# Motif terms of a Trainium2 kernel: neighbour planes replaced sixteen at a time by indirect gathers from DRAM, in place of a second buffer and moves within SBUF

## The chip, the cores and the metric

The kernel runs on one NeuronCore of one Trainium2 chip, as one program. The metric is the device time of one execution in microseconds (us). Data are float32 images of 2 x 128 x 128 x 96.

## What is computed

For each of the two images the reference adds a channel attention block to a group-normalised input, and then adds a "motif" block. Only the motif block bears on the change. It reads the image of shape 128 x 128 x 96 as 128 planes (feature channels) of 128 rows and 96 columns, in 16 groups of 8 planes:

```python
slices = [feature[:, :, ki:ki + Hm, kj:kj + Wm] for ki in range(K) for kj in range(K)]   # K = 3: nine shifts
patches = jnp.stack(slices, axis=2)
motif = patches.reshape(B, G, Cg * 9, L).reshape(B, G, 9, Cg, L)                         # G = 16, Cg = 8
gram = jnp.einsum('bgjcl,bgjdl->bgjcd', motif, motif)
...
nn_idx = jnp.argmin(d2, axis=-1)
u_max = jnp.max(nn_idx, axis=-1)
c_max = jnp.sum(nn_idx == u_max[..., None], axis=-1).astype(feature.dtype)
motif_nn = jnp.take_along_axis(motif, u_max[..., None, None], axis=3)
term = jnp.floor(motif * motif_nn * c_max[..., None, None] / Cg)
out_ser = motif * batch_mask + term
ser2 = out_ser.reshape(B, G, 9 * Cg, L).reshape(B, G, Cg, 9, Hm, Wm)
for k in range(K * K):
    ki, kj = (k // K, k % K)
    out = out.at[:, :, :, ki:ki + Hm, kj:kj + Wm].add(ser2[:, :, :, k])
```

The 72 patches of a group (9 shifts of 8 planes) are regrouped as nine blocks of eight. Each block picks one neighbour patch, which depends on the data. The last reshape counts the same 72 patches by plane and shift, so at output shift k, plane p takes the term of patch 9p + k, whose block is (9p + k) // 8 = p + (p + k) // 8. The block, and with it the neighbour plane, is the same for shift after shift, and changes once, at k = 8 - p.

## The kernel before, in words

For each of the two images (b = 0, 1) three stages follow one another: `attention`, `motif_grams` (the Gram matrices, the distances, and the choice of the neighbours) and `motif_terms` (the terms and their sum). A barrier stands between stages. The change lies in `motif_terms`.

**Layout.** Each of the 128 SBUF partitions holds one plane (partition 8g + p is plane p of group g). The planes lie in DRAM in `f_dram`. They are worked on in N = 8 slabs of R = 16 rows. Per slab there is `fc` (the plane's own rows, a plain load of 768 KB) and `near` (the neighbour plane's rows, 18 rows, gathered by an indirect DMA whose per-partition offset is in `index`). Both have four slots, by slab modulo 4.

**Steps.** `steps` takes slabs in pairs: for a pair (2m, 2m + 1) it runs shift 0 of both slabs, then shift 1 of both, up to shift 8. These are 72 steps an image, numbered n. Step n and step n - 2 are the same slab at neighbouring shifts. Each step takes:

- VectorE, `product` (L1510): `prod` = shifted `fc` times `near`; and two steps later `overshoot` (L1611): `over` = (scale times `prod`) < `rnd`. The order on VectorE is product n, overshoot n - 2, product n + 1, and so on (`LAG` = 2).
- ScalarE, two activations (L1637, L1642) that round the scaled product to `rnd`.
- TensorE, 8 fp32 matmuls with the identity (L1663) and 4 bf16 matmuls with minus the identity (L1667), which sum `rnd` and `over` in PSUM.
- After shift 8 ScalarE copies the slab's sum out (`finish`, L1629), and GpSimd adds it to the output in DRAM with an accumulating DMA (`add_out`, L1563), at shift 2 of the next pair but for the last pair.

**The neighbour planes.** At shift `sh` the 16 partitions 8 - sh + 8g need another neighbour plane than before. The kernel gathers both: `near` with the first pick, and a second full buffer `near2` with the second pick. Before each step of shift 1 to 8 SyncE waits for the product of step n - 2 (`product_made`), then issues a DMA within SBUF from `near2` to `near` for those 16 partitions (L1541, 108 KB). `product_inputs` makes product n wait for it on `moved`. The gathers (`gather`, L1555) of slab i + 2 are issued by GpSimd after the products of slab i at shifts 1 and 3 (the two halves of `near`) and 5 and 7 (the two halves of `near2`). SyncE's queue also holds the `fc` loads (L1528) of slab i + 2, at shift 5. The first two slabs' `near` and `near2` are gathered whole as the stage begins.

All of SyncE's DMAs go out in the order of its program, and so do GpSimd's: each waits behind what stands ahead of it in its engine's list. `on_pool` is False for every step, so that GpSimd only issues DMAs here (and two small memsets).

Of the kernel before, what the change touches and what calls it, by code (L numbers as in the profile page):

```python
# [1013 lines left out]
def motif_grams(nc, b, k, img, x_after, f_dram, x1_rows, x1_out, att_sems, sems):  # L1014
# [15 lines left out]
    with ExitStack() as ctx:  # L1030
# [23 lines left out]
        sel = sb("sel", [MG, 6, KK], F32)  # L1054
        block_picks = sb("block_picks", [MG, 3, KK], F32)
        both = sb("both", [P, 2, 3, KK], F32)
# [390 lines left out]
def motif_terms(nc, b, k, x, f_dram, out, gram_sems):  # L1447
# [10 lines left out]
    with ExitStack() as ctx:  # L1458
        sb = lambda n, s, d: ctx.enter_context(nc.sbuf_tensor(f"{n}{b}", s, d))
        sem = lambda n: ctx.enter_context(nc.semaphore(f"{n}{b}"))  # L1460
        near = sb("near", [P, SLOTS, NR * C], F32)
        near2 = sb("near2", [P, SLOTS, NR * C], F32)
        fc = sb("fc", [P, SLOTS, R * C], F32)
# [6 lines left out]
        scale = sb("scale", [P, KK], F32)  # L1470
        index = sb("index", [P, 2, 2, N], I32)
        acc = [ctx.enter_context(nc.psum_tensor(f"acc{s}_{b}", [P, R // BR, 512], F32)) for s in range(2)]
        (own, scaled, indexed, edged, prod_v, prod_p, rm_done, rnd_done, over_done, acc_done, out_ready) = (
            sem(n) for n in ("t_dve", "scaled", "indexed", "edged", "prod_v", "prod_p", "rm_done",
                             "rnd_done", "over_done", "acc_done", "out_ready"))
        stored, near_in, near2_in, fc_in = ([sem(f"{n}{j}_") for j in range(SLOTS)]
                                            for n in ("stored", "near_in", "near2_in", "fc_in"))
        moved = [sem(f"moved{s}_") for s in range(2)]
# [9 lines left out]
        def product_made(eng, n):  # L1488

            eng.wait_ge(prod_p if on_pool[n] else prod_v, sum(p == on_pool[n] for p in on_pool[:n + 1]))  # L1490
# [34 lines left out]
        @block.sync  # L1525
        def _(sp):
            def load_rows(dst, src, i, sem_):
                sp.dma_start(dst[:, i % SLOTS, :], src[:, R * i * C:(R * i + R) * C]).then_inc(sem_[i % SLOTS], 16)  # L1528

            if b + 1 < B:  # L1530
                for s_ in gram_sems.values():
                    sp.sem_clear(s_)
            for i in range(2):
                load_rows(fc, f_dram, i, fc_in)
            for n, (i, sh) in enumerate(steps):
                if sh >= 1:

                    if sh == 1:
                        sp.wait_ge(near2_in[i % SLOTS], landings(i))
                    product_made(sp, n - 2)  # L1540
                    sp.dma_start(near[MC - sh:P:MC, i % SLOTS, run(i)], near2[MC - sh:P:MC, i % SLOTS, run(i)]  # L1541
                                 ).then_inc(moved[i % 2], 16)
                if sh == 5 and i + 2 < N:
                    if i >= 2:
                        product_made(sp, number[(i - 2, KK - 1)])
                        product_made(sp, number[(i - 2, KK - 2)])
                    load_rows(fc, f_dram, i + 2, fc_in)
            for j in range(SLOTS):
                sp.wait_ge(stored[j], 16 * (N // SLOTS))

        @block.gpsimd
        def _(pool):
            def gather(i, second, cells, h=0):
                s = i % SLOTS
                pool.indirect_dma_start(  # L1555
                    (near2 if second else near)[:, s, cells], None, f_dram.rearrange("y (e o) -> (y e) o", o=1),
                    bass.IndirectOffsetOnAxis(ap=index[:, second, h, i:i + 1], axis=0)
                ).then_inc((near2_in if second else near_in)[s], 16)

# [7 lines left out]
            pool.wait_ge(indexed, 1)  # L1567
            for second in range(2):
                gather(0, second, run(0))
                gather(1, second, run(1))  # L1570
            pool.wait_ge(indexed, 2)
            for n, (i, sh) in enumerate(steps):
                if sh in (1, 3, 5, 7) and i + 2 < N:
                    product_made(pool, n)
                    if sh == 1 and i + 2 == N - 1:
                        nc.gpsimd.memset(near[:, (i + 2) % SLOTS, R * C:NR * C], 0.0).then_inc(edged, 1)
                    h = sh // 2 % 2
                    gather(i + 2, sh // 4, part_run(i + 2, h), h)
                if i >= 2 and sh == 2:
                    add_out(i - 2)  # L1580
                if on_pool[n]:
                    product_inputs(pool, n)
                    product(nc.gpsimd, n).then_inc(prod_p, 1)
# [4 lines left out]
        def _(dve):  # L1588
# [4 lines left out]
            for h in range(2):  # L1593
                nc.vector.scalar_tensor_tensor(index[:, :, h, :], offset[:, :].unsqueeze(2).to_broadcast([P, 2, N]),  # L1594
                                               float(HALF * C * h),
                                               k["row_base"][:, :].unsqueeze(1).to_broadcast([P, 2, N]), ALU.add,
                                               ALU.add).then_inc(indexed, 1)

# [73 lines left out]
def build(nc, x, w_qkv, b_qkv, w_dw, b_dw, temperature, w_out, b_out, out):  # L1672
# [5 lines left out]
    with ExitStack() as ctx:  # L1678
# [5 lines left out]
            minus_round=sb("minus_round", [P, 1], F32), group_planes=sb("group_planes", [MG, P], F32),  # L1684
            own_block=sb("own_block", [P, 2, KK], F32), pick=sb("pick", [P, 2, 3], F32),
            same_head=sb("same_head", [C, C], F32), same_block=sb("same_block", [MR, MR], F32),
# [45 lines left out]
```

## Time and profile before

| | us |
|---|---|
| median of 3 runs (lowest to highest) | 1575.14 (1575.06 to 1578.28) |
| the profiled execution, its own time | 1579.09 |
| span of its profile | 1577.1 |
| `motif_terms` of image 0 in it | about 513 to 788 |
| `motif_terms` of image 1 in it | about 1304 to 1577 |

The profile is that of one execution. Its time and its span differ by 2.0 us, which lie around the span. Engines are named PE (TensorE matmul), PEld (its weight load), DVE (VectorE), ACT (ScalarE), POOL (GpSimd) and SP (SyncE); a q behind a name is the engine's sequencer. An L with a number is a line of the kernel. "near<-near" is the move from `near2` to `near`, as the trace leaves numbers off the names of buffers. In a list of instructions, the part in brackets is the time that the engine was idle before it, and what ended the idle time.

### The profile page before, as it was taken

How to read it: one execution, taken by the hardware profiler on the slowest of the kernel's cores; microseconds unless marked ns; L12 is line 12 of the kernel's file. 1: busy time of each engine (PE TensorE's matmuls, PEld its weight loads, DVE VectorE, ACT ScalarE, POOL GpSimd, SP SyncE). 2: the span in 40 equal slices, each digit the busy share in tenths (PEclk: the TensorE clock that was granted, in tenths of full speed). 3: DMA queues.
4: the chain of work that ended last, by engine and by line, in shares of the span. 5: the costliest groups of instructions: out<-in, count | busy, mean ns of one | idle time of the engine just before them, and what ended most of it. 6: DMA issues, size and time to landing. Idle time of an engine off the chain costs nothing. (4 is left out here: it accounts for less than half of the span.)

```text
span 1577.1 us, 33962 instructions
## 1 busy us (share of the span) xinstructions
PE 1338.1 (85%) x13569; PEld 1079.0 (68%) x13569; DVE 1144.1 (73%) x1903; ACT 879.2 (56%) x950; POOL 680.3 (43%) x680
## 2 busy tenths in 40 slices
PE   0799999996988699999767887889978986999996
PEld 0699887985987355555356777888968983555553
DVE  8577675468864699999645565663786856999995
ACT  1455563212541699999634444542215526999995
POOL 3698892452220335440057566752533303354400
PEclk9999999898999799999969898997989997999998
DMA  6366631792141546453236655423901415464432
GB/s 224 88 209 203 195 90 32 212 273 93 42 168 75 180 123 178 100 142 72 52 101 182 182 155 169 126 62 101 273 5 70 193 62 172 131 178 100 142 72 51
DMA packets 78850, 208.12 MB, mean 132 GB/s; under 512 B 15633, under 2 KB 19827, under 8 KB 76035
## 3 DMA queue, kind: packets, MB, share of 16 engines
q1 hardware_dynamic: 64228, 153.09, 31.5%
q0 software_dynamic: 7296, 40.08, 9.9%
q10 hardware_dynamic: 7168, 12.78, 3.0%
q8 instruction: 107, 1.75, 0.5%
q14 instruction: 51, 0.42, 0.1%
HBM read 89.39 MB, written 67.04 MB: 99 GB/s over the span
## 5 line engine op out<-in xcount | busy, mean ns | idle before, releaser
L1663 PE MATMUL acc<-rnd,ident 128*128 128x376 f32 x1152 | 391.6, 483 | 24.7 <-ACT rnd L1642 24.7
L886 PE MATMUL ps_a<-wa,xa 128*128 128x192 f16 x1536 | 305.3, 251 | 12.7 <-DVE y_s L615 12.5
L1663 PEld LDWEIGHTS acc<-rnd,ident 128*128 128x128 f32 x1152 | 216.5, 192 | 145.3 <-ACT rnd L1642 26.0
L886 PE MATMUL ps_a<-wb,xb 128*128 128x192 f16 x1536 | 303.7, 250 | 0.0
L1510 DVE TENSOR_TENSOR prod<-fc,near 128x1504 f32<-128x1504 f32 x144 | 247.3, 1717 | 33.1 <-DMA near<-f_planes,index 17.4
L1637 ACT ACTIVATE rnd_m<-prod,plus_round,scale 128x1504 f32<-128x1504 f32 x144 | 235.8, 1637 | 61.6 <-DVE prod L1510 51.0
L549 POOL TENSOR_TENSOR vt<-z 96x256 f32<-96x256 f32 x248 | 256.6, 1055 | 18.7 <-ACT z L790 18.6
L1611 DVE SCALAR_TENSOR_TENSOR over<-prod,scale,rnd 128x1504 bf16<-128x1504 f32 x144 | 255.5, 1777 | 0.0
L1555 POOL DMA_INDIRECT near<-f_planes,index x56 | 159.0, 2840 | 209.8 <-DVE prod L1510 201.8
L1642 ACT ACTIVATE rnd<-rnd_m,minus_round 128x1504 f32<-128x1504 f32 x144 | 223.2, 1550 | 4.8
L886 PEld LDWEIGHTS ps_a<-wa,xa 128*128 128x128 f16 x1536 | 154.1, 100 | 19.7 <-issue 18.2
L886 PE MATMUL ps_a<-wfb,xb 128*128 128x96 f16 x1536 | 159.4, 207 | 1.7 <-issue 1.7
L886 PE MATMUL ps_a<-wfa,xa 128*128 128x96 f16 x1536 | 159.4, 208 | 1.2 <-issue 1.2
L886 PEld LDWEIGHTS ps_a<-wb,xb 128*128 128x128 f16 x1536 | 154.0, 100 | 0.9 <-issue 0.2
L557 POOL TENSOR_TENSOR td<-side 128x192 f32<-128x192 f32 x128 | 99.0, 774 | 120.5 <-ACT side L808 120.5
L886 PEld LDWEIGHTS ps_a<-wfa,xa 128*128 128x128 f16 x1536 | 141.8, 99 | 0.6 <-issue 0.6
L886 PEld LDWEIGHTS ps_a<-wfb,xb 128*128 128x128 f16 x1536 | 139.7, 99 | 2.3 <-issue 2.2
L1149 ACT ACTIVATE turned_hi<-ps_m 126x768 f16<-126x768 f16 x102 | 79.9, 810 | 90.9 <-PE ps_m L1200 90.9
L886 PE MATMUL ps_a<-wc,xc 102*128 102x192 f16 x512 | 128.8, 251 | 0.0
L1667 PE MATMUL acc<-over,minus_ident 128*128 128x376 bf16 x576 | 117.0, 326 | 8.8 <-DVE over L1611 8.6
L609 DVE TENSOR_TENSOR td<-side 128x192 f32<-128x192 f32 x128 | 73.9, 577 | 66.7 <-ACT side L808 63.6
L815 ACT ACTIVATE qk<-y_s 128x384 f16<-128x384 f32 x128 | 66.9, 523 | 92.0 <-DVE y_s L615 92.0
(304 smaller groups left out, 2390.3 us busy)
## 6 DMA issues: line engine op xcount, KB each, us to landing
xb<-xa ACTq DMA_DIRECT2D x64, 195.0 KB, 2.7
f_planes<-img SPq DMA_DIRECT2D x8, 1536.0 KB, 14.0
fc<-f_planes SPq DMA_DIRECT2D x16, 768.0 KB, 5.5
out<-done_rows POOLq DMA_DIRECT2D x16, 768.0 KB, 8.2
v_a<-xa SPq DMA_DIRECT2D x40, 260.0 KB, 2.7
v_b<-xb SPq DMA_DIRECT2D x40, 260.0 KB, 3.2
xa<-v_a SPq DMA_DIRECT2D x40, 260.0 KB, 4.9
xb<-v_b SPq DMA_DIRECT2D x40, 260.0 KB, 5.5
```

The costliest lines, as they stand in the source:

```text
L549: last = nc.gpsimd.tensor_tensor(out[:, i], row(p_), row(q_), op)
L557: nc.gpsimd.tensor_tensor(td[:, n % 2, 0], side[:, n % 2, 0], side[:, n % 2, 1], ALU.add).then_inc(t_made, 1)
L609: nc.vector.tensor_tensor(td[:, s, 1], side[:, s, 0], side[:, s, 1], ALU.subtract).then_inc(d_made, 1)
L886: mm = lambda a, w, first, end: nc.tensor.matmul(out(i), a, w, start=first, stop=end)
L1149: last = nc.scalar.activation(columns(turned_hi[q % 2], col), six(ps_hi[u % 2]), ACT.Copy)
L1510: return vec.tensor_tensor(prod[:, n % PRODS], fv, nv, ALU.mult)
L1555: pool.indirect_dma_start((near2 if second else near)[:, s, cells], None, f_dram.rearrange("y (e o) -> (y e) o", o=1), bass.IndirectOffset ...
L1611: nc.vector.scalar_tensor_tensor(over[:, n % 2], prod[:, n % PRODS], scale[:, sh:sh + 1], rnd[:, n % RNDS], ALU.mult, ALU.is_lt).then_inc( ...
L1637: nc.scalar.activation(rnd_m[:, n % 2], prod[:, n % PRODS], ACT.Identity, bias=k["plus_round"][:, 0:1], scale=scale[:, sh:sh + 1]).then_in ...
L1642: nc.scalar.activation(rnd[:, n % RNDS], rnd_m[:, n % 2], ACT.Identity, bias=k["minus_round"][:, 0:1]).then_inc(rnd_done, 1)
L1663: nc.tensor.matmul(o(m), k["ident"][:, :], rnd[:, n % RNDS, BR * m:BR * m + BR, :], start=False, stop=False, skip_group_check=True)
L1667: last = nc.tensor.matmul(o(m), k["minus_ident"][:, :], over[:, n % 2, BR * m:BR * m + BR, :], start=False, stop=(sh == KK - 1), skip_grou ...
```

## The change

`near2` and the moves go. The planes that change at a shift are gathered from DRAM by GpSimd, 16 at a time, straight into their rows of `near`. The offsets of these gathers are in a new table `index2` with 16 partitions (one per group), 8 columns by shift and one value for each slab, which VectorE computes at the start of the stage from `block_picks`; that tensor becomes a global one. The gathers of slab i + 2 are now two (at shifts 2 and 5), each placed behind the replacement of the same step, and no longer wait for product n. SyncE keeps only the `fc` loads.

```diff
-        block_picks = sb("block_picks", [MG, 3, KK], F32)
+        block_picks = k["block_picks"]
...
-        near2 = sb("near2", [P, SLOTS, NR * C], F32)
...
-        index = sb("index", [P, 2, 2, N], I32)
+        index = sb("index", [P, 2, N], I32)
+        index2 = sb("index2", [MG, MC, N], I32)
+        base2 = sb("base2", [MG, 2], F32)
+        offset2 = sb("offset2", [MG, MC], F32)
...
@@ @block.sync
             for n, (i, sh) in enumerate(steps):
-                if sh >= 1:
-
-                    if sh == 1:
-                        sp.wait_ge(near2_in[i % SLOTS], landings(i))
-                    product_made(sp, n - 2)
-                    sp.dma_start(near[MC - sh:P:MC, i % SLOTS, run(i)], near2[MC - sh:P:MC, i % SLOTS, run(i)]
-                                 ).then_inc(moved[i % 2], 16)
                 if sh == 5 and i + 2 < N:
...
@@ @block.gpsimd
+            planes = f_dram.rearrange("y (e o) -> (y e) o", o=1)
+
+            def gather(i, cells, h=0):
+                pool.indirect_dma_start(near[:, i % SLOTS, cells], None, planes,
+                                        bass.IndirectOffsetOnAxis(ap=index[:, h, i:i + 1], axis=0)
+                                        ).then_inc(near_in[i % SLOTS], 16)
+
+            def replace(i, sh):
+
+                lines = slice(MC - sh, P, MC)
+                pool.indirect_dma_start(near[lines, i % SLOTS, run(i)], None, planes,
+                                        bass.IndirectOffsetOnAxis(ap=index2[:, MC - sh, i:i + 1], axis=0)
+                                        ).then_inc(moved[i % 2], 16)
...
             pool.wait_ge(indexed, 1)
-            for second in range(2):
-                gather(0, second, run(0))
-                gather(1, second, run(1))
-            pool.wait_ge(indexed, 2)
+            gather(0, run(0))
+            gather(1, run(1))
+            pool.wait_ge(indexed, 3)
             for n, (i, sh) in enumerate(steps):
-                if sh in (1, 3, 5, 7) and i + 2 < N:
-                    product_made(pool, n)
-                    if sh == 1 and i + 2 == N - 1:
+                if sh >= 1:
+                    product_made(pool, n - 2)
+                    replace(i, sh)
+                if sh in (2, 5) and i + 2 < N:
+                    if sh == 2 and i + 2 == N - 1:
                         nc.gpsimd.memset(near[:, (i + 2) % SLOTS, R * C:NR * C], 0.0).then_inc(edged, 1)
-                    h = sh // 2 % 2
-                    gather(i + 2, sh // 4, part_run(i + 2, h), h)
+                    gather(i + 2, part_run(i + 2, sh // 5), sh // 5)
                 if i >= 2 and sh == 2:
                     add_out(i - 2)
...
@@ @block.vector
             for h in range(2):
-                nc.vector.scalar_tensor_tensor(index[:, :, h, :], offset[:, :].unsqueeze(2).to_broadcast([P, 2, N]),
-                                               float(HALF * C * h),
-                                               k["row_base"][:, :].unsqueeze(1).to_broadcast([P, 2, N]), ALU.add,
-                                               ALU.add).then_inc(indexed, 1)
+                nc.vector.tensor_scalar(index[:, h, :], k["row_base"][:, :], offset[:, 0:1], float(HALF * C * h),
+                                        ALU.add, ALU.add).then_inc(indexed, 1)
+            c.then_wait(nc.vector.tensor_scalar(base2[:, 0:1], k["plane_f"][0:MG, :], float(MC * PLANE), None, ALU.mult))
+            nc.vector.scalar_tensor_tensor(base2[:, 1:2], k["group_base"][0:MG, :], float(MC), base2[:, 0:1], ALU.mult,
+                                           ALU.add)
+            c.then_wait(nc.vector.scalar_tensor_tensor(offset2[:, :], k["block_picks"][:, 0, 1:KK], float(PLANE),
+                                                       k["block_picks"][:, 1, 1:KK], ALU.mult, ALU.add))
+            for i in range(N):
+                last = nc.vector.tensor_scalar(index2[:, :, i], offset2[:, :], base2[:, 1:2], float(first_row(i) * C),
+                                               ALU.add, ALU.add)
+            last.then_inc(indexed, 1)
```

## Rows read from the trace of the kernel before

**Rows 1.** The page: span, and the engines in 40 equal slices.
```profile
span 1577.1 us, 33962 instructions
...
PE   0799999996988699999767887889978986999996
...
DVE  8577675468864699999645565663786856999995
```
**Rows 2.** Busy time by stretch, in the steady part of each `motif_terms`.
```profile
core 0: us, PE busy (x) PEld busy (x) DVE busy (x) ACT busy (x) POOL busy (x), PEclk, DMA share, GB/s
...
1322.00:1564.00 242.00, 238.37 (x883) 132.24 (x883) 234.81 (x141) 230.32 (x147) 82.21 (x32) 1.00 0.42 110
532.00:775.00 243.00, 237.87 (x879) 131.68 (x878) 235.25 (x141) 230.93 (x147) 81.56 (x31) 1.00 0.42 110
```
**Rows 3.** What DVE waited for, 510 to 788, then 1304 to 1577 us.
```profile
DVE prod L1510 <- DMA near<-f_planes,index: 9.6, 2, 8.2
DVE prod L1510 <- DMA near<-near: 8.6, 5, 2.9
...
DVE prod L1510 <- DMA near<-f_planes,index: 7.8, 2, 7.4
DVE prod L1510 <- DMA near<-near: 7.0, 5, 3.1
```
**Rows 4.** Line L1541, the moves: issue to landing, whole span.
```profile
L1541 SPq DMA_DIRECT2D near<-near x128: 486/487/531, 527.5 to 1549.1; - x128
...
DMA to landing us min/median/max: 2.0/2.2/7.3
```
**Rows 5.** Instructions in order of time, DVE and POOL, 1333 to 1342 us.
```profile
1334.67 1.77 DVE L1611 SCALAR_TENSOR_TENSOR over<-prod,scale,rnd 128x1504 bf16<-128x1504 f32 x1
1335.02 3.88 POOL L1555 DMA_INDIRECT near<-f_planes,index  x1 [7.75 <-DVE prod L1510]
1336.36 1.71 DVE L1510 TENSOR_TENSOR prod<-fc,near 128x1504 f32<-128x1504 f32 x1
...
1338.00 1.77 DVE L1611 SCALAR_TENSOR_TENSOR over<-prod,scale,rnd 128x1504 bf16<-128x1504 f32 x1
1339.20 3.02 POOL L1555 DMA_INDIRECT near<-f_planes,index  x1 [0.30 <-issue]
1339.69 1.71 DVE L1510 TENSOR_TENSOR prod<-fc,near 128x1504 f32<-128x1504 f32 x1
```
**Rows 6.** The same view, POOL alone: DVE idle, then image 0's second gather after step 2.
```profile
1309.09 0.94 POOL L1555 DMA_INDIRECT near<-f_planes,index  x1 [0.30 <-issue]
...
535.53 2.26 POOL L1555 DMA_INDIRECT near<-f_planes,index  x1 [1.07 <-DVE prod L1510]
```
**Rows 7.** The same view, 1388 to 1402 us: a gather beside a DVE gap.
```profile
1388.88 1.95 POOL L1563 DMA_DIRECT2D out<-done_rows  x2
...
1394.63 1.78 DVE L1611 SCALAR_TENSOR_TENSOR over<-prod,scale,rnd 128x1504 bf16<-128x1504 f32 x1
...
1394.99 2.39 POOL L1555 DMA_INDIRECT near<-f_planes,index  x1 [4.17 <-DVE prod L1510]
...
1397.64 1.73 DVE L1510 TENSOR_TENSOR prod<-fc,near 128x1504 f32<-128x1504 f32 x1 [1.23 <-DMA near<-near]
```
**Rows 8.** Line L1555 in 535 to 536 us: one half gather, its landing from issue.
```profile
L1555 POOL DMA_INDIRECT near<-f_planes,index x1: 2259/2259/2259, 535.5 to 535.5; - x1
...
DMA to landing us min/median/max: 5.4/5.4/5.4
```
**Rows 9.** Busy time by stretch around two adds and the third and fourth gathers, image 0.
```profile
598.00:602.00 4.00, 4.00 (x18) 2.48 (x17) 4.00 (x4) 3.97 (x3) 3.31 (x3) 1.00 0.77 194
602.00:606.00 4.00, 4.00 (x16) 2.38 (x15) 4.00 (x3) 3.93 (x4) 0.51 (x1) 1.00 0.93 187
606.00:608.00 2.00, 2.00 (x10) 1.09 (x9) 0.91 (x1) 2.00 (x2) 1.88 (x1) 1.00 1.07 242
608.00:610.00 2.00, 2.00 (x9) 1.25 (x8) 0.81 (x1) 1.81 (x2) 0.00 (x0) 1.00 1.05 230
610.00:612.00 2.00, 0.79 (x3) 0.19 (x1) 2.00 (x2) 1.05 (x1) 0.81 (x1) 1.00 0.79 245
```
**Rows 10.** The tile `index`: the DVE operations that write it.
```profile
L1594 DVE SCALAR_TENSOR_TENSOR index<-offset,row_base x4: 166/172/176, 513.6 to 1304.8; 128x16 int32<-128x16 f32 x4
```

More of the change, by code:

```diff
@@ L1475, in motif_terms @@
                              "rnd_done", "over_done", "acc_done", "out_ready"))
-        stored, near_in, near2_in, fc_in = ([sem(f"{n}{j}_") for j in range(SLOTS)]
-                                            for n in ("stored", "near_in", "near2_in", "fc_in"))
+        stored, near_in, fc_in = ([sem(f"{n}{j}_") for j in range(SLOTS)] for n in ("stored", "near_in", "fc_in"))
         moved = [sem(f"moved{s}_") for s in range(2)]
@@ L1552, in _ @@
         def _(pool):
[L1553 to L1558, printed above, removed]
+            planes = f_dram.rearrange("y (e o) -> (y e) o", o=1)
[8 more added lines that the diff above has]
+                                        ).then_inc(moved[i % 2], 16)
             def add_out(i):
@@ L1684, in build @@
             minus_round=sb("minus_round", [P, 1], F32), group_planes=sb("group_planes", [MG, P], F32),
-            own_block=sb("own_block", [P, 2, KK], F32), pick=sb("pick", [P, 2, 3], F32),
+            own_block=sb("own_block", [P, 2, KK], F32), block_picks=sb("block_picks", [MG, 3, KK], F32), pick=sb("pick", [P, 2, 3], F32),
             same_head=sb("same_head", [C, C], F32), same_block=sb("same_block", [MR, MR], F32),
```

## The prediction

> **What bounds the kernel now.** I read the page first, for the two stretches where DVE and PE are both near 9 tenths [rows 1]: these are the two `motif_terms` stages. Busy time by stretch then shows that in 242 us PE is busy for 238.4, DVE for 234.8 and ACT for 230.3, at full granted clock, while POOL is busy for 82 [rows 2]. Three engines run in step, and none has room to catch up: what DVE loses, PE loses too, and the end moves by as much. The list of instructions gives the cadence: product to product 3.33 us (1336.36 to 1339.69), and from a product's end (1338.07) to the next product's start 1.62 us, in which one `over` runs [rows 5]. The waits say what DVE lacks beside that: 9.6 and 7.8 us for the first gathers of a stage, and 8.6 and 7.0 us for the moves [rows 3]. The moves are nearly always hidden: they land 2.2 us after their issue [rows 4], and product n starts 1.62 + 3.33 = 4.95 us after the end of product n - 2, which releases its move. **So 4.95 us is the whole room** from product n - 2 to the landing of what product n needs. The question is what a gather on POOL takes of it.
>
> **What is removed.** 64 moves an image, with the waits for them: 8.6 us in image 0 and 7.0 in image 1, 15.6 in all. 28 gather issues an image become 14, which were off the path (POOL idle for most of the stage). Half of the gathered bytes come back as the 64 replacements of 108 KB, so DRAM traffic is unchanged; with a DMA share of 0.42 [rows 2] I give the freed SBUF traffic nothing.
>
> **What is added, off the path.** DVE gets 11 more small operations at the stage's start; the one that writes `index` takes 0.17 us [rows 10], so some 2 us with their waits. They stand behind the operation that releases the first gather, in the 7.4 to 8.2 us that DVE waits for it [rows 3]: nothing. Without that cover they would cost these 2 us an image.
>
> **What is added, on the path: the replacement's issue.** With DVE idle an indirect issue takes 0.94 us. With DVE busy it takes 3.88 us from 1335.02 to 1338.90, and the next 3.02 us, from 1339.20 to 1342.22. Both end 0.82 us after the end of a product (1338.07, 1341.40) [rows 5, 6]. Where DVE pauses, one takes 2.39 us and ends at 1397.38, 0.97 us after the `over` that ended at 1396.41 [rows 7]. The two direct DMAs of the adds take 0.98 us each beside a busy DVE [rows 7]. I read this as follows: the issue must read its list of offsets, gets no turn while DVE runs one instruction on the heels of the last, gets one at a product's end or in a pause, and then needs 0.8 us. How much of that goes with the number of partitions no row shows; bounds are 0 and 0.97, and I take 0.8, since all issues seen, of whole and half gathers, need about that.
>
> **From the issue's end to the landing.** A half gather (442 KB) lands 5.4 us from its start, 5.4 - 2.26 = 3.1 after the issue's end [rows 8]. A move (the same 16 partitions and bytes, but on SP and from SBUF) lands 2.2 - 0.49 = 1.7 after [rows 4]. These are the bounds; I take 2.0, nearer to the move, which has the same size. By the Trainium skill, page "DMA: Bandwidth & Descriptors", section "Anatomy of one DMA — SWDGE (gpsimd) path", a DMA from GpSimd costs 2.0 us plus its bytes at 436 GB/s; an estimate from it is 2.25 us here, and each wait below would be 0.25 us longer. No run here shows it.
>
> **The steady wait.** Replacement n is issued after product n - 2, so POOL starts under `over`, misses the boundary behind it, and gets its turn at the end E of product n - 1. It lands at E + 0.8 + 2.0 = E + 2.8, where product n could have started at E + 1.62: DVE waits 1.2 us. This wait is a pause. Replacement n + 1, already queued, gets its turn in it, behind the `over`: it is done at about E + 1.7 + 0.8 and lands at E + 4.5, before product n + 1 is due at E + 2.8 + 3.33. So every second step waits: 32 of an image's 64, and 32 x 1.2 = 38.4 us. By the bounds (0 + 1.7 and 0.97 + 3.1, less 1.62) a wait is 0.1 to 2.4 us.
>
> **The queue at shift 2.** POOL's list is now replacement, gather, add for the even slab, and then the same for the odd one. The odd slab's replacement stands behind 442 KB and an add, and shares their queue. How long: around the adds the DMA engines are full from 600 to 611 us [rows 9], some 11 us for two adds, a gather and the last part of another (1.5 us each), so some 4 us an add. In image 0 a move on its own queue waited up to 7.3 us there [rows 4]. POOL finishes the first add's issue at about E + 3.6; gather and add occupy the queue to about E + 8.0; the replacement behind lands at E + 10.0 (2.0 later), where its product was due at E + 2.8 + 3.33 = E + 6.1: 3.9 us. The next one, behind the second gather and add, costs 2.6. Less the 1.2 counted already, that is 5.3 for two pairs of slabs, and 1.5 for the last, which has no gathers: 12 us an image. Bounds: 0, if the queue doesn't hold the replacement back, and 20.
>
> **The start.** SP, rid of its waits, issues `fc` loads 2 and 3 at once, beside the second gather; against that `near2` no longer stands before the first replacement. I take 1 us lost, between a gain of 2 and a loss of 3.
>
> **Sum.** Image 0: 38.4 + 12 + 1 - 8.6 = +42.8. Image 1: 38.4 + 12 + 1 - 7.0 = +44.4. Together +87 on a span of 1577.1 and an own time of 1579.1. On the median, 1575.1, that gives **1662 us**. A measurement of this kernel can tell about 0.2% (3 us) from no change. With the waits at 0.3 us and the queue's cost halved it is 1575 + 2 x (10 + 6 + 1) - 16 = 1593; with 2.0 us and 16 us, 1575 + 2 x (64 + 16 + 1) - 16 = 1721.
>
> **Rival 1: the turn comes at the end of whatever DVE runs.** Then an issue starting 0.28 us after a product's end is through behind the `over`, in 2.26 us as at 535.53 [rows 6], and lands at 0.28 + 2.26 + 2.0 = 4.5 us, inside 4.95. No steady wait; the queue at shift 2 and the start stay: 2 x 13 - 15.6 = +10, 1586 us. For it: that one row. Against it: 3.88 us in the steady rows [rows 5], where the issue went past the end of an `over` at 1336.44. This is also what the Trainium skill says on the page "SBUF — State Buffer", section "Who interferes with whom": a VectorE instruction with two SBUF inputs contends with a GpSimd one that reads SBUF, and the second blocks until the first finishes. By that rule the trace agrees that DVE's instructions hold the issue up, and disagrees on where it ends. Chance 0.17.
>
> **Rival 2, the other side: faster.** The issue for 16 partitions is cheap. It decides at 4.95 - 0.28 - 2.0 = 2.67 us of issue: below that nothing waits in the steady part; and if a queued replacement also passes beside the adds, all waits for moves are gone and nothing replaces them: 1575.1 - 15.6 = 1559.5 us. For it: the 0.94 us with DVE idle, and the few rows at 2.3 [rows 6, 7]. Against: the steady rows, and that it must hold in both places. Chance 0.11.
>
> **Rival 3: every step waits.** If the pause gives POOL no turn, or a landing takes 3 us and more, both slabs' replacements are late: 2 x (64 x 1.2 + 13) - 15.6 = +164, 1739 us. Against it: the pause at 1396.41 did give a turn [rows 7]. Chance 0.07. My forecast has 0.65.
>
> **Range and chances.** 1580 to 1710 leaves out rival 2, rival 3 and the edge of rival 1, some 2 in 10. Faster comes from rival 2, 0.11; within 0.2%, 0.03, from the bounds of rival 1; slower 0.86.
>
> **What would show it.** Right: DVE waits for `near` from an indirect DMA some 30 times an image, 1.2 us each, mostly ahead of even slabs' products; indirect issues of two kinds, near 3.8 and near 2 us; POOL busy for over half of the stage; two waits of 2 to 4 us at shift 2 of pairs 2 to 4. Wrong: issues of 16 partitions well under 2 us beside a busy DVE (rival 2), all near 2.3 us (rival 1), waits at odd slabs as well (rival 3), or a granted clock below full in the steady part, which I have priced at nothing because a PE pause of over a microsecond left it at 1.00 [rows 9].

## The result and the profile after

The changed kernel takes 1610.69 us (median of 4 runs, 1609.07 to 1613.03) against 1575.1 us (4 runs of the kernel before on the same chip): a ratio of 1.0235, 95% interval 1.0194 to 1.0277. It is slower by some 36 us, where 87 were forecast. The profiled execution took 1609.07 us, with a span of 1607.3.

The page of the changed kernel, its span and two engines in 40 slices (compare [rows 1]):

```profile
span 1607.3 us, 33940 instructions
...
PE   0799999996985989899568877989959958988996
...
DVE  8577774588843989899544554763786839988985
```

Busy time by stretch, changed kernel, in 243 and 250 us of the two stages (compare [rows 2]):

```profile
532.00:775.00 243.00, 229.85 (x829) 125.79 (x828) 224.27 (x135) 220.21 (x140) 143.98 (x78) 0.98 0.31 80
1340.00:1590.00 250.00, 234.59 (x851) 130.38 (x849) 229.74 (x138) 224.41 (x143) 144.48 (x78) 0.98 0.31 78
```

PE, DVE and ACT each lose 8 to 11 us of the 243; POOL rises from 82 to 144. The DMA share falls from 0.42 to 0.31, as the moves are gone. DVE's waits, 510 to 790, then 1303 to 1607 us (compare [rows 3]):

```profile
DVE prod L1511 <- DMA near<-f_planes,index: 29.1, 14, 6.5
...
DVE prod L1511 <- DMA near<-f_planes,index: 30.7, 13, 7.9
```

Before, they were 18.2 and 14.8 in all. A `motif_terms` stage, counted from DVE's first operation in it (`offset`) to the end of its barrier, took 275.1 and 272.6 us before (547.7 together) and takes 291.4 and 291.8 (583.2); "stages" below gives this sum. **So the stages lose 35.5 us**: 26.8 in DVE's waits, 4.0 at the barriers (below), 4.7 elsewhere. Of these 4.7 us, 3.3 are the changed kernel's additional small operations of DVE at the start, 1.6 us in image 0 and 1.7 in image 1 (from `offset` to the last `scale` 0.9 us before, 2.5 here): they stand where DVE had waited for the first gather, whose wait is counted shorter by them. The untouched stages vary between single executions (1029.4 before, 1024.1 here, 1012 to 1030 over all the profiles), so single executions are compared by this stage sum.

Where the 29.1 us of image 0 stand: 10.5 at the start (6.50, 2.24, 1.42, 0.36), 15.6 at shifts 2 and 3 of pairs 2 to 4 (3.80 + 2.69, 4.53 + 2.24, 1.36 + 1.00), 2.6 at shift 1 of the same pairs (0.84, 0.93, 0.85), and 0.3 more. The steady part, for which 38.4 us were forecast, has nothing. Instructions in order of time there, changed kernel, DVE and POOL:

```profile
558.93 1.77 DVE L1619 SCALAR_TENSOR_TENSOR over<-prod,scale,rnd 128x1504 bf16<-128x1504 f32 x1
559.28 2.13 POOL L1557 DMA_INDIRECT near<-f_planes,index  x1 [1.19 <-DVE prod L1511]
560.62 1.72 DVE L1511 TENSOR_TENSOR prod<-fc,near 128x1504 f32<-128x1504 f32 x1
```

The replacement's issue begins 0.35 us into an `over`, as the gather at 1335.02 in [rows 5] did, but is through at 561.41, 0.71 us after the end of that `over` (560.70), where the gather went on to 0.82 us after the next product. The line's summary, whole span:

```profile
L1557 POOL DMA_INDIRECT near<-f_planes,index x128: 847/2134/3770, 518.9 to 1578.8; - x128
...
DMA to landing us min/median/max: 2.6/4.0/8.2
```

With 0.28 + 4.0 = 4.3 us the median landing is inside the room of 4.95.

### The profile page after: what moved, and what is told of

It reads as the page before. It is cut to its first block and busy times, and to the rows that moved or that the text cites. A ratio compares the mean times of both kernels' runs of the same rounds, so it can differ in the third digit from the quotient of the medians.

```text
span 1607.3 us, 33940 instructions
## 1 busy us (share of the span) xinstructions
PE 1342.4 (84%) x13569; PEld 1077.6 (67%) x13569; DVE 1148.5 (71%) x1925; ACT 880.3 (55%) x950; POOL 816.4 (51%) x780
## 5 line engine op out<-in xcount | busy, mean ns | idle before, releaser
L1671 PE MATMUL acc<-rnd,ident 128*128 128x376 f32 x1152 | 398.6, 490 | 26.8 <-ACT rnd L1650 26.8
L1557 POOL DMA_INDIRECT near<-f_planes,index x128 | 254.5, 1988 | 212.0 <-DVE prod L1511 201.3
L1671 PEld LDWEIGHTS acc<-rnd,ident 128*128 128x128 f32 x1152 | 220.7, 195 | 151.0 <-ACT rnd L1650 28.1
L886 PE MATMUL ps_a<-wa,xa 128*128 128x192 f16 x1536 | 307.8, 253 | 12.7 <-DVE y_s L615 12.2
L1675 PEld LDWEIGHTS acc<-over,minus_ident 128*128 128x128 bf16 x576 | 48.1, 99 | 124.7 <-DVE over L1619 95.4
```

The lines of the kernel that those rows point to most:

```text
L886: mm = lambda a, w, first, end: nc.tensor.matmul(out(i), a, w, start=first, stop=end)
L1557: pool.indirect_dma_start(near[lines, i % SLOTS, run(i)], None, planes, bass.IndirectOffsetOnAxis(ap=index2[:, MC - sh, i:i + 1], axis=0)) ...
L1671: nc.tensor.matmul(o(m), k["ident"][:, :], rnd[:, n % RNDS, BR * m:BR * m + BR, :], start=False, stop=False, skip_group_check=True)
L1675: last = nc.tensor.matmul(o(m), k["minus_ident"][:, :], over[:, n % 2, BR * m:BR * m + BR, :], start=False, stop=(sh == KK - 1), skip_grou ...
```

## The experiments

**Is it the order in which products are released?** In the changed kernel a replacement lands, and so releases its product, only while the `over` ahead of that product runs; in the kernel before the move lands earlier. First, the kernel before with its moves released later:

```diff
                     product_made(sp, n - 2)
+                    if n >= 4:
+                        sp.wait_ge(over_done, n - 3)
                     sp.dma_start(near[MC - sh:P:MC, i % SLOTS, run(i)], near2[...]
```

> The kernel before, in which SyncE issues the move for step n only once overshoot n - 4 is done as well, 1.7 us later than now; the move then lands some 4.1 us after the end of product n - 2, still ahead of the 4.95 us at which product n is due. Theory A (order of release: GpSimd gets its turn at the first end of a VectorE instruction at which VectorE's next one had not yet been released when GpSimd asked): the next product is now released only after GpSimd asked, so the half gathers' issues fall from 3.0 and 3.9 us to about 2.3 and 1.5 us. Theory B (issues over 16 partitions are quicker than issues over 128): nothing changes, 3.0 and 3.9 us. Time by either within 10 us of the kernel before.

1591.16 us, stages 568.0: DVE waited 17.0 us for moves in each image, so the time isn't within 10 us of before, as both theories had it (22 more). The gathers were mixed. POOL's list, this kernel:

```profile
543.13 3.89 POOL L1557 DMA_INDIRECT near<-f_planes,index  x1 [8.42 <-DVE prod L1510]
547.33 3.03 POOL L1557 DMA_INDIRECT near<-f_planes,index  x1 [0.30 <-issue]
556.46 2.26 POOL L1557 DMA_INDIRECT near<-f_planes,index  x1 [6.10 <-DVE prod L1510]
```

So 128 partitions can be quick too, and neither theory predicts the mixture. What the three rows leave out: behind the third one's `over` DVE paused (its next product, at 558.86, waited 0.97 us for a move), behind the first two it didn't. Second, the changed kernel with its replacements sent to a spare tile that nothing waits for:

```diff
-            else:
-                eng.wait_ge(moved[i % 2], 16 * (8 * (i // 2) + sh))
...
-                pool.indirect_dma_start(near[lines, i % SLOTS, run(i)], None, planes,
+                if 8 * (i // 2) + sh > 1:
+                    pool.wait_ge(moved[i % 2], 16 * (8 * (i // 2) + sh - 1))
+                pool.indirect_dma_start(spare[lines, i % 2, run(i)], None, planes,
```

> The changed kernel, but the 16 planes are gathered into a spare buffer that nothing reads, and the products do not wait for them (the planes that change at a shift are thus left out of the result). Same issues, same partitions, same bytes. Theory A: products are released early, GpSimd loses its turn at the end of the overshoot, and the issues over 16 partitions take about 3.8 and 3.0 us in place of 2.1. Theory B: they stay at 2.1 us. VectorE's waits fall to those for the first two gathers, some 9 us an image; time about 1610 - 2 x 20 = 1570 us.

1570.49 us, stages 543.4, so the issues and their traffic cost next to nothing by themselves: the loss is in who waits. (The waits are 12.2 us below those of the kernel before and the barriers 4.0 above, which with the 3.3 us of small operations makes 542.8.) In image 0 the issues that began 0.35 us into an `over` took 2.13 us through pair 0, and from 585.80 on most took 3.02 to 3.77, with the same 16 partitions and with products released equally early in both. Release order and the number of partitions therefore can't be what makes the difference.

```profile
552.49 2.14 POOL L1558 DMA_INDIRECT spare<-f_planes,index  x1 [1.19 <-DVE prod L1510]
...
585.80 3.77 POOL L1558 DMA_INDIRECT spare<-f_planes,index  x1 [7.86 <-DVE prod L1510]
589.88 3.03 POOL L1558 DMA_INDIRECT spare<-f_planes,index  x1 [0.30 <-issue]
```

**The queue at shift 2.** No adds for slabs 0 to 5, nor the waits for them:

```diff
-                if i >= 2 and sh == 2:
-                    add_out(i - 2)
```

> The changed kernel without the accumulating DMAs of slabs 0 to 5 of each image (those slabs lack the motif sum in the output); the last two adds stay. Theory (queue at shift 2: the replacement stands behind gather and add on GpSimd's queue): VectorE's waits at shifts 2 and 3 of pairs 2 to 4 (15.6 and 16.9 us) go, as a half gather alone costs 0 to 0.4 us; time about 1610 - 32 = 1578 us. Rival (the gathers, or the issue times on GpSimd, make these waits): at least a third of them, 10 us over both images, stays, 1588 us or more.

1575.79 us, stages 550.5: 32.7 us less, and the waits at shifts 2 and 3 of pairs 2 to 4 are gone but for 0.3 us. In the changed kernel this is the stretch. POOL and DVE in order of time:

```profile
590.97 1.02 POOL L1564 DMA_DIRECT2D out<-done_rows  x1
592.29 1.94 POOL L1557 DMA_INDIRECT near<-f_planes,index  x1 [0.30 <-issue]
594.53 1.48 POOL L1550 DMA_INDIRECT near<-f_planes,index  x1 [0.30 <-issue]
596.00 1.01 POOL L1564 DMA_DIRECT2D out<-done_rows  x1
597.32 0.92 POOL L1557 DMA_INDIRECT near<-f_planes,index  x1 [0.30 <-issue]
598.94 1.73 DVE L1511 TENSOR_TENSOR prod<-fc,near 128x1504 f32<-128x1504 f32 x1 [3.80 <-DMA near<-f_planes,index]
...
605.05 1.73 DVE L1511 TENSOR_TENSOR prod<-fc,near 128x1504 f32<-128x1504 f32 x1 [2.69 <-DMA near<-f_planes,index]
```

The replacement issued at 597.32 took only 0.92 us of POOL, in DVE's pause, but its line's summary gives its landing at 7.7 us: 6.8 after the issue's end, where 1.7 to 1.9 is usual. It stands behind 768 KB of add. Cutting each add in four keeps the work and spreads it:

```diff
-                if i >= 2 and sh == 2:
-                    add_out(i - 2)
+                if i >= 2 and sh in (3, 4, 6, 7):
+                    add_out(i - 2, 4 * (3, 4, 6, 7).index(sh), 4)
```

> The changed kernel with each add of slabs 0 to 5 cut in four (4 rows, 192 KB each), issued at shifts 3, 4, 6 and 7, behind that step's replacement, not beside the half gathers of shifts 2 and 5. Theory (queue): a quarter of an add holds its queue for about 1 us, against the 0.7 us that a replacement has to spare, so most of the 32.5 us of waits at shifts 2 and 3 goes; 0 to 0.5 us is left for each quarter. Time about 1611 - 28 = 1583 us, still slower than the kernel before by 0.2 to 1%. Rival (the number of bytes in the queue matters, not where they stand): the waits spread out and stay, 1600 us or more. The barrier at a stage's end lags the last landing by 1.5 us with 36 DMAs of GpSimd in a stage and 3.5 with 86; if it goes by their number, it is about 4.2 us here with 104.

1578.83 us, ratio to before 1.0033 (1.0006 to 1.0059), stages 553.3: the waits at shifts 2 and 3 are gone here too, and the change is then worth nothing, or slightly less. The same cut in the kernel before (at shifts 2, 4, 6, 8, behind product n):

> The kernel before with each add of slabs 0 to 5 cut in four, issued at shifts 2, 4, 6 and 8 after the product of the step (its half gathers stand at 1, 3, 5 and 7). If the adds' load on the DMA engines is what makes the moves at shifts 2 to 4 late (5.7 and 4.0 us of waits), most of these waits go: 7 to 9 us faster than the kernel before, ratio 0.994 to 0.996, 1566 us beside a median of 1575. If the moves are late for another cause: no change. The barrier's lag by the number of GpSimd DMAs (54): 2.2 us, against 1.5.

1568.06 us, ratio 0.996 (0.993 to 0.999), stages 541.9: **faster than both kernels**, than the one before by 0.4%. The waits for moves behind the start fall from 5.7 to 1.8 us in image 0 and from 4.0 to 1.9 in image 1. DVE's waits in this kernel, 510 to 800:

```profile
DVE prod L1510 <- DMA near<-near: 4.7, 3, 2.8
DVE prod L1510 <- DMA near<-f_planes,index: 9.7, 2, 8.2
```

**The start.** `fc` loads 2 and 3 held back until product (i, 4):

> The changed kernel, but SyncE issues the fc loads of slabs 2 and 3 only after the products of slabs 0 and 1 at shift 4, as late as in the kernel before. If the early loads slow the second gather, VectorE's wait before its second product (2.2 and 2.1 us) falls to the 1.4 and 0.4 us of the kernel before, and the waits of the next two products shrink too: 2 to 4 us less over both images, about 1607 us. If not, the same as the changed kernel, 1610 us, with the same waits.

1599.98 us, but stages 583.1, the same as 583.2, so the rest of the difference in time is in the untouched stages (1015.0 against 1024.1). The early loads did slow the first gathers: held back, the second product's wait fell from 2.24 to 1.13 us and from 2.05 to 0.31, and in image 1 the first gather landed 8.4 us after `offset` instead of 10.4, and the first product came at 8.47 instead of 10.45. All waits of the start together fell from 10.5 to 8.0 and from 10.9 to 8.7 us. But new waits at shift 5 (1.1 and 1.6 us) and growth in others took as much. Not a lever.

**How near the edge is it?** A memset on POOL ahead of each replacement, 1000 and then 2000 elements a partition (0.93 and 1.8 us):

```diff
                     product_made(pool, n - 2)
...
+                    nc.gpsimd.memset(pad[:, :], 0.0).then_inc(padded, 1)
...
                     replace(i, sh)
```

> The changed kernel with a GpSimd memset of 128 x 1000 fp32 (about 0.9 us) between the wait for product n - 2 and the replacement of step n, so that GpSimd asks for its turn 0.9 us later, after the previous replacement has landed and the next product has been released, but still before the end of the overshoot. Theory A: it loses the turn at the end of the overshoot; the issue ends after the next product, 1.7 us later, and VectorE waits 1 us or more at every second step: some 30 us or more an image, 1670 us. Rival (the turn always comes at the end of the overshoot): the memset is covered by the overshoot, and the time stays within 10 us of 1610.

1616.19 us, stages 596.2. The issue begins 1.2 us into an `over` and is still through behind it, although its product had been released before it asked: by release order it should have lost this turn, and the time been near 1670. The 13 us more are further waits of DVE, 0.8 to 0.9 us each, most of them at steps where a gather also stands in POOL's list. DVE and POOL in order of time:

```profile
539.84 1.78 DVE L1626 SCALAR_TENSOR_TENSOR over<-prod,scale,rnd 128x1504 bf16<-128x1504 f32 x1
541.06 1.27 POOL L1560 DMA_INDIRECT near<-f_planes,index  x1 [0.15 <-POOL pad L1580]
543.31 0.93 POOL L1580 MEMSET pad<- 128x1000 f32 x1 [0.98 <-DVE prod L1514]
```

> As the kernel with the memset ahead of each replacement, but 128 x 2000 (1.8 us), so that GpSimd asks only about 0.5 us after the overshoot's end, while the next product runs. Then the forecast's regime must come about whatever decides a turn within the overshoot: the issue ends 0.7 us after the end of product n - 1, lands at E + 0.7 + 1.8 = E + 2.5 where product n was due at E + 1.6, and VectorE waits 0.9 us at every second step or more often: 25 to 60 us an image above the changed kernel's waits, 1660 to 1730 us. If the time stays within 10 us of the changed kernel, the room of 4.95 us is not what bounds a replacement.

1722.4 us, stages 698.2: now the request falls just behind the `over`, the turn comes at the product's end, and 58 of an image's 72 products wait, most of them 0.7 to 1.0 us. That is near the forecast's 1.2 for an issue that gets its turn there (with 0.71 and 1.9 us for its 0.8 and 2.0 it is 0.71 + 1.9 - 1.62 = 1.0). Instructions in order of time, POOL and DVE; the issue ends at 658.84, 0.72 us behind the product's end (658.12):

```profile
653.75 1.78 DVE L1626 SCALAR_TENSOR_TENSOR over<-prod,scale,rnd 128x1504 bf16<-128x1504 f32 x1
656.39 1.73 DVE L1514 TENSOR_TENSOR prod<-fc,near 128x1504 f32<-128x1504 f32 x1 [0.86 <-DMA near<-f_planes,index]
656.51 2.33 POOL L1560 DMA_INDIRECT near<-f_planes,index  x1 [0.16 <-POOL pad L1580]
658.03 1.78 DVE L1626 SCALAR_TENSOR_TENSOR over<-prod,scale,rnd 128x1504 bf16<-128x1504 f32 x1
660.69 1.73 DVE L1514 TENSOR_TENSOR prod<-fc,near 128x1504 f32<-128x1504 f32 x1 [0.88 <-DMA near<-f_planes,index]
```

A missed turn is therefore as dear as forecast. What was wrong is that it is missed.

**Why 3.88 us before and 2.13 after?** I sorted the indirect issues of the profiles by how long ago the last one had ended. Of those that begin 0.35 us into an `over` that a product follows without a pause, the kernel before has 18 that come 6.1 to 12.8 us after it: all 18 go past the end of the `over`. It has 6 that come up to 3.3 us after it: all 6 are through behind it. The changed kernel has 6 with 7.85 us, all long, and 75 with up to 4.2 us, all short. The 7.85 us are the two steps of shift 0, without a replacement; the issue behind them is the one at shift 1 that costs 0.8 to 0.9. Changed kernel, POOL and DVE in order of time:

```profile
579.46 3.77 POOL L1557 DMA_INDIRECT near<-f_planes,index  x1 [7.85 <-DVE prod L1511]
585.05 1.72 DVE L1511 TENSOR_TENSOR prod<-fc,near 128x1504 f32<-128x1504 f32 x1 [0.84 <-DMA near<-f_planes,index]
```

Four runs set out to test this (theory C in the expectations).

```diff
+            def touch():
...
+                if touches[0] > 0:
+                    pool.wait_ge(touched, 16 * touches[0])
+                pool.indirect_dma_start(spare[0:MG, ...], None, planes, ...).then_inc(touched, 16)
...
+                if sh == 0 and n >= 2:
+                    product_made(pool, n - 2)
+                    touch()
```

> The changed kernel, with one tiny indirect DMA (16 x 96 elements into a spare tile) added at each step of shift 0, behind product n - 2, where POOL otherwise issues nothing for 7.85 us. Theory C (recency): an indirect issue that starts under an over gets its turn at that over's end if POOL's last indirect issue ended within about 4.2 us, and only at the next product's end if it ended 6 us ago or more; in the kernel before 6 of 6 and 18 of 18 issues go by this, in the changed one 75 of 75 and 6 of 6. Then the six issues of 3.77 us become 2.13, their waits of 0.8 to 0.9 us go (5.2 us in all), and the two stages take 583 - 5 + 0.5 (the barrier's 6 more DMAs) = 579 us. Rival (it is the shift 1, or its place in the code, that makes the issue long): 3.77 us and the waits stay, 583 us and more.

> The kernel before, with the same tiny indirect DMA behind the product of every step at which GpSimd issues no gather, so that POOL has a turn every 3.3 us. Theory C: all gathers of 128 partitions issue in about 2.25 us, none in 3.88; the time stays within 10 us of the kernel before, as these issues are off the path. Rival (gathers of 128 partitions into near and near2 miss the over's end for another reason): 3.88 us as before, 18 times.

> The changed kernel with the adds in four parts at shifts 3, 4, 6 and 7 and the tiny indirect DMAs at shift 0. Theory C: the waits of 13.5 and 14.5 us of the version with split adds lose 2.6 each; against that some 0.3 us a stage for the barrier's additional DMAs: stages 553.3 - 4.6 = 549 us, the same as the kernel before (547.7 and 0.2% either way). Rival: 553 to 554.

1611.92 us (ratio 1.0282, 1.0227 to 1.0337), 1586.65 and 1574.92 (ratio 1.004, 1.0016 to 1.0063); stages 584.3, 565.1 and 548.5. The first two missed: waits at shift 1 stayed in part (0.91, none and 0.23 us in image 0), and gathers of the second took 3.15 and 3.02 us. My tiny issues waited for the landing of the one before and so started late, with the gathers queued behind them, some 1.1 us into an `over`. These two don't decide. The third met its number, but with two of image 0's three waits at shift 1 still there (0.87 us each), so that is partly luck. The fourth thins the turns out:

```diff
                     product_made(pool, n - 2)
-                    replace(i, sh)
+                    if sh % 2 == 0 and i % 2 == 0:
+                        replace(i, sh)
```

> The changed kernel that keeps only the replacements of even slabs at shifts 2, 4, 6 and 8, so that 13.3 us lie between them (or 6.66 from a gather at shift 5); the other 48 of an image's 64 are left out, and the terms that need them are not the reference's. Theory C: those at shifts 2, 4 and 8 take 3.77 us (those behind a gather less than 4.2 us ago 2.13), land late, and DVE waits 0.8 to 0.9 us for each such one: some 3 a pair, 12 an image, so about 10 us an image for 16 replacements, though POOL does a quarter of the work. Rival (fewer issues can only be quicker): all 2.13 us, no wait but those at shifts 2 and 3 behind the adds.

1585.08 us, stages 561.3. Image 0 has 12 long issues and 12 waits behind its start, 0.74 to 1.02 us each and 10.6 in all: as theory C had it in number and sum, and in place too but for one: none at shift 2 of the first pair, which is in the stage's start, and one at shift 6 of the last, which has no gather at shift 5. (They begin 0.5 us later in the `over`, so "long" is 3.28.) Three of the four short ones follow a gather by 1.1 us, the other is in the stage's start. POOL in order of time, this kernel (the first row is a gather):

```profile
547.35 2.25 POOL L1550 DMA_INDIRECT near<-f_planes,index  x1 [1.07 <-DVE prod L1511]
550.68 2.15 POOL L1557 DMA_INDIRECT near<-f_planes,index  x1 [1.08 <-DVE prod L1511]
564.51 3.28 POOL L1557 DMA_INDIRECT near<-f_planes,index  x1 [11.68 <-DVE prod L1511]
585.35 3.26 POOL L1557 DMA_INDIRECT near<-f_planes,index  x1 [17.56 <-DVE prod L1511]
```

Then the tiny issues again, each into a slot of its own, without waits:

> As the version with tiny indirect DMAs at the steps of shift 0, but each goes into a slot of its own, so that it doesn't wait for the landing of the one before (that wait had put its start off by 1.5 us and queued the next replacement behind it). Theory C: an issue that starts under an over gets its turn at the over's end if the turn before was also at an over's end and less than 4.4 us ago (698 of 698 issues so far). Then the six issues of 3.77 us become 2.13, the waits of 0.8 to 0.9 us at shift 1 go (5.2 us in all), and the stages take 583 - 5 + 0.5 = 579 us. Rival (the place in the code or the shift): 3.77 us and the waits stay.

> The kernel before with tiny indirect DMAs behind the product of every step without a gather, each into a slot of its own and without waits. Theory C: after the start of the stage the issues of gathers, 3.88 us long 18 times before, take 2.25 us. Rival (gathers of 128 partitions miss the over's end for another reason): 3.88 us, 18 times.

> The changed kernel with the adds in four parts and the tiny unwaited indirect DMAs at shift 0. Theory C: the waits of 13.5 and 14.5 us of the version with split adds become 11 to 12, against 0.3 us a stage for the barrier: stages 549 us, the time 4 us below that version's 1578.8, still not below the kernel before. Rival: stages 553.

In the first (1604.76 us, stages 582.3) no issue takes over 2.5 us any more and the waits at shift 1 are gone; DVE's waits fall by 2.6 us in all, not 5.2, as other waits grew, and the stages by 0.9, not 4. So the length of the issues came out as theory C had it, the time did not. POOL at the place of the 3.77:

```profile
578.20 2.15 POOL L1572 DMA_INDIRECT spare<-f_planes,index  x1 [1.19 <-DVE prod L1514]
581.53 2.14 POOL L1560 DMA_INDIRECT near<-f_planes,index  x1 [1.18 <-DVE prod L1514]
```

In the second, the kernel before, all 56 gathers are short; first its own list, then its line's summary:

```profile
537.95 2.27 POOL L1558 DMA_INDIRECT near<-f_planes,index  x1 [1.17 <-DVE prod L1513]
541.28 2.27 POOL L1558 DMA_INDIRECT near<-f_planes,index  x1 [1.06 <-DVE prod L1513]
```

```profile
L1558 POOL DMA_INDIRECT near<-f_planes,index x56: 938/2265/2296, 506.8 to 1472.6; - x56
```

The same gathers to the same tiles take 2.27 us if a turn precedes them, and 3.9 if none does. One run gave 1565.28 us, stages 551.0: nothing gained in them, as these issues were off the path, and 3.3 us lost, as much as the barrier takes for 47 more DMAs a stage (below). The third took 1580.0 us (ratio 1.0005, 0.9967 to 1.0043), stages 549.1 as expected; the 4 us in time are within its spread. The best form of the change is level with the kernel before and behind it with split adds (541.9).

**The barrier.** Line L1458, the end of the stage, changed kernel:

```profile
L1458 POOLq DRAIN  x2: 11053/11856/12658, 786.0 to 1596.0; - x2
L1458 SPq COMPARE_BRANCH  x2: 33/33/33, 795.2 to 1603.6; - x2
L1458 SPq DRAIN  x2: 7/7/7, 795.4 to 1603.8; - x2
L1458 SPq EVENT_SEMAPHORE  x2: 17/17/17, 798.8 to 1607.3; - x2
```

SP is past its last wait for a store at 795.2, and the barrier opens 3.6 us later, behind POOL's drain. Before, it opened 1.6 us after:

```profile
L1458 SPq COMPARE_BRANCH  x2: 33/33/33, 786.9 to 1575.4; - x2
L1458 SPq EVENT_SEMAPHORE  x2: 17/17/17, 788.5 to 1577.0; - x2
```

Over the kernels this lag goes with the DMAs that GpSimd issued in the stage: 1.6 us at 36, 2.3 at 54 (split adds before), 3.4 at 80, 3.6 at 86, 4.4 at 104, so about 0.04 us each. The version with sparse replacements, which is the changed kernel with 38, has 1.7.

## Why the prediction was right and wrong

**The bound** was right: with three engines in step, what DVE waited was lost (26.8 of the stages' 35.5 us), and the room of 4.95 us decided. The version with the longer memset lost some 0.9 us at most steps as soon as it was exceeded.

**"The steady wait" is the step that failed.** It said that POOL "misses the boundary behind it, and gets its turn at the end E of product n - 1". In the changed kernel the turn comes at the end of the `over`, and the landing inside the room; 38.4 us an image became 2.6, at shift 1 of three pairs. The step took 3.88 us [rows 5] as what an issue beside a busy DVE costs, and the row at 535.53 with 2.26 [rows 6] as the exception. The bracket of each row had the difference: 7.75 us idle ahead of the one, 1.07 ahead of the other. The forecast's own pattern, an issue every 3.3 us, is that of the second row.

**The issue's fixed part and the landing** were near: 0.71 us behind the boundary for 16 partitions (0.8 forecast), 1.7 to 1.9 us from issue end to landing where nothing stood ahead of it (2.0 forecast), 2.0 to 2.5 behind a half gather. The Trainium skill, page "DMA: Bandwidth & Descriptors", section "Anatomy of one DMA — SWDGE (gpsimd) path", gave an estimate of 2.25; the runs lie below it if counted, as there, from the issue's end; from the start of an issue with DVE idle, at 522.35, the landing came after 2.7.

**The queue at shift 2** was right in mechanism and size: 3.9 and 2.6 us forecast twice, 3.80 + 2.69 and 4.53 + 2.24 measured. Only the subtraction of "the 1.2 counted already" went with the failed step: 15.6 and 16.9 us instead of 12.

**The start** was forecast at about 2 us gained in waits (the 2.9 and 3.1 us of the moves there go, 1 is lost). Image 0 gained 2.0; image 1 gained nothing, and its first product came 10.45 us after `offset` where it had come after 8.25 (9.00 against 9.10 in image 0). The version with late `fc` loads shows why: without `fc` loads 2 and 3 beside the first gather it came at 8.47 (one execution; all ten other versions of the changed kernel had 10.45 to 10.69 there). The forecast had them beside the second gather alone. The 11 small operations cost nothing themselves, as forecast: they ended 6.5 and 7.9 us before the first gather's landing let DVE go on.

**Missing from the sum**: the barrier's 2.0 us a stage. The drain stood in the trace of before, but I priced no more than the waits in the loop.

**Rival 1** was what happened, in its mechanism, for all but the issues behind shift 0: no steady wait, queue and start stay. Its 1586 us lack the barrier (4.0), the full queue (8.5 more), the waits at shift 1 (5.2) and the start of image 1. It also cited the Trainium skill, page "SBUF — State Buffer", section "Who interferes with whom", by which the second instruction blocks until the first finishes. The 2.13 us rows agree with it; those of 3.77 and 3.88 don't, as there the issue waits through a second instruction. DVE's own products took 1.72 us in both kernels, so it was POOL alone that waited.

**The granted clock** was priced at nothing. It did dip. Busy time by stretch in the changed kernel, where PE had been idle for 3.56 us up to 602.42:

```profile
600.00:602.00 2.00, 0.00 (x0) 0.00 (x0) 2.00 (x2) 1.30 (x1) 1.06 (x1) 0.92 0.99 200
602.00:604.00 2.00, 1.58 (x5) 1.08 (x6) 0.36 (x1) 1.89 (x2) 1.09 (x1) 0.50 0.89 214
```

At 0.50 (1.2 of 2.4 GHz) PE's fp32 matmuls are dearer: those at 603.67 and 604.30 took 0.83 us, where 0.48 is usual. But the mean of all 1152 rose only from 483 to 490 ns, 7 us of busy time over both images and partly under DVE's own waits; how much it makes of the 1.4 us of the stages that are in no term was not tried.

## What to carry to other kernels

A duration beside a busy engine belongs to its history: sort the rows of an operation by the idle time in their brackets before taking one for a new, denser pattern. Small DMAs that a step waits for don't belong in one queue with a 768 KB accumulating store; cutting the store and spreading it paid in both kernels. When moving DMAs to GpSimd, price its drain at the stage's barrier too.

## What the hardware showed that was not expected

What follows is of indirect DMA issues on GpSimd that begin under an `over`. Such an issue gets its turn at the end of that `over` if the turn before was at an `over`'s end less than 4.4 us ago: nearly 700 issues up to the twelfth experiment, and 354 in the last three, without an exception. It gets its turn only at the end of the product behind the `over` if three things hold: the last indirect issue was 6 us or more ago, DVE had made no pause for 9 us, and that product follows the `over` without a pause. That was so for 71 of 72 in the kernels before, after and the first six experiments, and for 24 of 24 in the one with sparse replacements. A memset in between doesn't count as a turn: in the version with 1000 elements the six replacements behind shift 0 were long, though a memset had just ended.

Where an issue begins about 1.1 us into an `over`, behind one that had its turn at a product's end, both outcomes occur. Over all 17 profiles, all 98 behind whose `over` DVE paused were short. Of the others, 129 of 131 were long if the issue before had itself gone past the end of an `over`, and 30 of 201 if that one had begun under a product. What in the chip keeps this memory is open.
